# PSUM banks divided into two rings of four, tiled TensorE calls merged, and every engine's call list redrawn

## The reference

```
# 1. state-space block: in-projection, causal convolution over 4 tokens, then per head (8 heads of 64)
z, xBC, dt = split(x @ W_in.T)
y = sum over s<=l of (C_l . B_s) * exp(cum_l - cum_s) * (x_s * dt_s)     # the masked 256x256 matrix Lm
y = (y + x*D) * silu(z);  y = y * rsqrt(mean(y*y)) * norm_w
x1 = layernorm(x + y @ W_out.T)
# 2. attention: queries from x1, keys and values from the 120 context rows and the 256 rows of x1
x2 = layernorm(x1 + softmax(q k^T / 8) v @ Wout)
# 3. coupling network, three cycles, and a global network on the mean over tokens
gf = sigmoid(global_net(mean(x2)))
for 3 cycles: tf = sigmoid(w4 gelu(w3 gelu(w2 gelu(w1 h))));  h = h + coupling(gf, tf) * twist(h)
return layernorm(x2 + h)
```

## Time and profile before

| | |
|---|---|
| median of three runs | 3862.34 us |
| profiled execution: span from first to last instruction | 3861.4 us |
| between span and median | 0.9 us |
| matmul instructions | 25728 |
| TensorE busy | 3783.3 us, 98% |
| VectorE busy | 3286.2 us, 85% |
| ScalarE busy | 3237.9 us, 84% |
| GpSimd busy | 1748.5 us, 45% |
| mean granted TensorE clock | 0.992 of full |

### The profile page before, as it was taken

How to read it: one execution, slowest core, us unless ns; L and a number is a source line. 1 busy time by engine, 2 the same in 40 slices (tenths; PEclk the granted TensorE clock), 3 DMA queues, 4 the chain that set the end, 5 groups by cost and what they waited for, 6 DMA issues and landing times.

```text
span 3861.4 us, 77375 instructions
## 1 busy us (share of the span) xinstructions
PE 3783.3 (98%) x25728; PEld 3000.9 (78%) x25728; DVE 3286.2 (85%) x8098; ACT 3237.9 (84%) x7812; POOL 1748.5 (45%) x3084
## 2 busy tenths in 40 slices
PE   6999999999999999999999999999999999999997
PEld 5777877877877878778778778777787787787775
DVE  7888888888888888888888888888888888888874
ACT  5788888888888888888888888888888888888885
POOL 3444445354454444453544544534535445445442
PEclk8999999999999999999999999999999999999998
DMA  3111112111211111121111111111211211111110
GB/s 97 54 47 59 55 45 61 54 42 58 58 45 55 48 59 54 45 61 53 43 57 59 45 55 50 56 55 45 61 55 42 61 55 45 55 54 53 55 38 17
DMA packets 312350, 203.14 MB, mean 53 GB/s; under 512 B 55056, under 2 KB 310928, under 8 KB 311952
## 3 DMA queue, kind: packets, MB, share of 16 engines
q1 hardware_dynamic: 311952, 198.20, 17.5%
HBM read 180.17 MB, written 17.96 MB: 51 GB/s over the span
## 4 chain that ended last, share of the span: by engine, by line
PE 59%; ACT 16%; DVE 15%; issue 4%; POOL 4%; DMA 1%; SPq 0%; DVEq 0%; POOLq 0%
PE psum L253 20%; PE psum L428 8%; PE psum L338 6%; PE psum L463 5%; PE psum L438 5%; PE psum L452 4%; PE psum L325 4%; ACT prob L979 3%; ACT h L1021 2%; ACT L979 2%; ACT L1021 2%; PE psum L497 2%; ACT xc L891 2%; POOL rs_mix L2175 2%; DVE nmax L1638 1%
## 5 line engine op out<-in xcount | busy, mean ns | idle before, releaser
L979 ACT ACTIVATE prob<-psum,nmax 128x376 f32<-128x376 f32 x1024 | 585.2, 575 | 49.5 <-DVE nmax L1638 46.2
L1638 DVE TENSOR_REDUCE nmax<-psum 128x1 f32<-128x376 f32 x1024 | 541.5, 540 | 14.4 <-PE psum L428 11.0
L2139 POOL TENSOR_TENSOR Lm<-Lm,G 128x384 f32<-128x384 f32 x512 | 506.1, 1012 | 92.8 <-DVE out_sb L1741 68.4
L438 PE MATMUL psum<-ident,prob 128*128 128x128 f32 (+1 forms) x3072 | 480.5, 276 | 2.1 <-ACT probT L989 1.1
L1442 DVE SCALAR_TENSOR_TENSOR u<-psum,par,u 128x253 f32<-128x253 f32 (+5 forms) x960 | 449.1, 479 | 28.1 <-ACT u L882 1.7
L428 PE MATMUL psum<-kT,q_sb 64*128 64x376 f32 x2048 | 467.7, 528 | 0.2 <-ACT prob L979 0.2
L438 PEld LDWEIGHTS psum<-ident,prob 128*128 128x128 f32 (+1 forms) x3072 | 363.0, 141 | 73.9 <-issue 45.0
L989 ACT ACTIVATE probT<-psum 128x384 f32<-128x384 f32 x512 | 252.7, 494 | 182.7 <-PE psum L438 182.5
L2126 POOL TENSOR_SCALAR_AFFINE_SELECT Lm<-Lm 128x256 f32<-128x256 f32 x512 | 205.7, 435 | 411.6 <-DMA Lm<-cum_row 411.6
L253 PE MATMUL psum<-x_hi,w_in_hi 128*128 128x256 f32 (+1 forms) x1152 | 360.9, 313 | 22.5 <-DVE w_in_lo L1764 9.3
L452 PE MATMUL psum<-probT,V 128*64 128x256 f32 (+1 forms) x3072 | 375.0, 385 | 0.3 <-ACT probT L989 0.3
(11 more groups left out here) (222 smaller groups left out, 11157.9 us busy)
## 6 DMA issues: line engine op xcount, KB each, us to landing
Lm<-cum_row SPq DMA_DIRECT2D x64, 1024.0 KB, 5.2
Lm<-cum_row SPq DMA_DIRECT2D x64, 512.0 KB, 6.5
invT<-inv_row SPq DMA_DIRECT2D x256, 128.0 KB, 3.0
xT_sb<-in_xT SPq DMA_DIRECT2D x64, 256.0 KB, 3.1
x_sb<-in_x SPq DMA_DIRECT2D x64, 256.0 KB, 3.3
result<-out_sb SPq DMA_DIRECT2D x64, 256.0 KB, 2.2
inv_row<-inv_t SPq DMA_DIRECT2D x512, 1.0 KB
ctx_sb<-in_ctx SPq DMA_DIRECT2D x64, 120.0 KB, 2.7
```

Of the source, the lines that this page charges most:

```text
L438: t = tr(banks[b][0:m, j * P:(j + 1) * P], prob[:, r, j0:j0 + m], ident[:, :])
L979: act(prob[:, r, :], b[:, 0:NK], ACT.Exp, bias=nmax[:, n:n + 1], accum_out=psum_row[:, n:n + 1]).then_inc(a_exp, 1)
L1638: e.tensor_reduce(nmax[:, n:n + 1], banks[bank_of["sc", s, n]][:, 0:NK], AX.X, ALU.max, negate=True).then_inc(d_max, 1)
L2139: t = tt(Lm[:, h, :], Lm[:, h, :], G[:, :], ALU.mult)
```

## The change

**Banks.** `scores` go round four banks (`RING_S`); every other call of TensorE goes round the other four (`RING_O`), the coupling network included.

**Larger calls.** `scores(s, c)` makes the four products of a head pair in one call instead of two in each of two. `y_half(s, d)` replaces two `y_pair` and puts both results side by side in one bank; `values(s, d)` replaces two `values` likewise. The readers (`y_out` on DVE, `values_out` on ACT) wait until both halves of the bank are written.

**Lists.** All five engines' lists are drawn anew. The loop is still over `p` from 2 to 62, but TensorE's now starts at another point: the second and third cycle of the coupling network of `m - 3` and the last six `turn`s and last `values` of `f` stand at the head of a turn of the loop. The products of all calls are the same, 25728 matmul instructions by the same sizes.

```
-        ring_turn = (4, 5)
+        RING_S, RING_O = (0, 1, 2, 3), (4, 5, 6, 7)
...
-            ring_s, ring_b, ring_m = [1, 2, 3], list(ring_turn), [6, 7]
+            ring_s, ring_o = list(RING_S), list(RING_O)
...
-                b = bank_of["x", s, j] = take(ring_m)
+                b = bank_of["x", s, j] = take(ring_o)
...
-                b = bank_of["tn", s, n] = take(ring_b)
+                b = bank_of["tn", s, n] = take(ring_o)
...
+            def y_half(s, d):
...
+                b = bank_of["y", s, d] = take(ring_o)
                 pe.wait_ge(d_xdt, 2 * s + 2)
+                for q in (2 * d, 2 * d + 1):
+                    pe.wait_ge(l_Lm, 4 * s + q + 1)
+                    o = q % 2 * L
+                    for i, (c0, c1, m0) in enumerate(((0, L, 0), (P, L, L))):
+                        for k in range(2):
+                            h = 2 * q + k
+                            t = mm(banks[b][k * HD:(k + 1) * HD, o + c0:o + c1], xdt[:, i, h * HD:(h + 1) * HD],
+                                   Lm[:, h, m0:m0 + c1 - c0], start=i == 0, stop=i == 1)
+                    t.then_inc(p_y, 1)
+                freed[b] = [(d_yD, 4 * s + 2 * d + 2)]
...
+            def scores(s, c):
...
+                for i in range(TT):
+                    for k in range(2):
+                        n = 2 * (TT * c + i) + k
+                        b = bank_of["sc", s, n] = take(ring_s)
...
+                        freed[b] = [(a_exp, 16 * s + n + 1)]
...
+            def values(s, d):
...
+                for c in (2 * d, 2 * d + 1):
+                    pe.wait_ge(a_tn, 8 * s + 2 * c + 2)
+                    pe.wait_ge(d_tn, 8 * s + 2 * c + 2)
...
+                freed[b] = [(a_o, 4 * s + 2 * d + 2)]
...
-                b = wait_free(0)
+                at = bank_of["f", s, cyc, n] = take(ring_o)
+                b = banks[at]
...
-                sc.wait_ge(p_val, 4 * s + c + 1)
+                sc.wait_ge(p_val, 4 * s + c // 2 * 2 + 2)
...
-                ve.wait_ge(p_y, 4 * s + q + 1)
+                ve.wait_ge(p_y, 4 * s + q // 2 * 2 + 2)
```

More of the change, by code:

```diff
@@ L705, in _ @@
+            layer(last - 3, 1, 2)
+            turn(last - 2, 14)
+            turn(last - 2, 15)
+            layer(last - 3, 1, 3)
+            k_tile(last - 1, 1)
+            k_tile(last - 1, 2)
+            in_z(last, 1)
+            layer(last - 3, 2, 1)
+            q_pair(last - 1, 1)
+            layer(last - 3, 2, 2)
+            values(last - 2, 1)
+            v_tile(last - 1, 0)
             k_tile(last - 1, 3)
+            layer(last - 3, 2, 3)
+            scores(last - 1, 1)
+            turn(last - 1, 0)
@@ L1002, in x2_out @@
                     return
+                b = banks[bank_of["x2T", s]]
                 sc.wait_ge(p_f, FP * s + 1)
```

1479 lines of the change are left out of this document (730 added, 749 removed).

## The result

The changed kernel takes 4058.62 us (median of four runs, 4056.83 to 4061.93) against 3862.67 for the kernel before beside it: a ratio of 1.0507, with a 95% interval of 1.0492 to 1.0522. The direction was forecast, the size was not: 3909 us was the value, 3985 the upper end of the range, and +196 us is over four times the +46 of the sum. The profiled execution has a span of 4055.0 us and a mean granted clock of 0.993.

The account below looks back on a forecast made before the run. TensorE was taken as the bound. Per sequence, -1.35 (visits) + 2.4 (table loads) + 0.3 (banks) - 0.6 (old waits) = +0.75 us, over about 62 sequences +46 us: 3909 us; own range 3870 to 3950, eight in ten 3795 to 3985.

Parts of the forecast that it names:

- TensorE bounds; less work there without new waits is the gain: TensorE is 98% busy at full clock, so the kernel needs less TensorE work per sequence without new waits there.
- Visits, 1.35 us, at most 1.56: Merged scores, values and y calls make fewer trips to half arrays on TensorE, saving 0.96 to 1.56 us per sequence.
- Five loads in one chain, 2.4 us: ScalarE's 10.75 us from in_x to glob(f, 0), against TensorE's 8.39, makes TensorE wait about 2.4 us at glob(f, 1).
- Faster: Rival: TensorE already waits elsewhere in that stretch, halving the glob(f, 1) wait, and visits return their upper price; 3802 us, chance 0.30.
- The four shared banks, 0.3 us, between 0 and 0.6: Calls outside scores wait for the reader of the fourth call before; 0.3 us per sequence allowed, at turn(f, 15).
- the place named as tight: turn(f, 15) takes the bank of turn(f, 12), which DVE reads behind out_norm; 0.3 us, between 0 and 0.6.
- Where readers come at once, nothing waits: At the shared banks, full-array calls between take 0.4 to 1.5 us and a reader 0.5, so no wait.
- Much slower: Rival: the four-bank ring in strict order lets late DVE readers, such as gate_silu, stop TensorE; 3982 us, chance 0.13.
- GpSimd's and the DMAs' other orders, nothing: New orders for POOL, 46% busy, and the DMA queues, 18%, were counted at nothing.
- Old waits go, -0.6 us: TensorE's estimated 0.6 us of true waits per sequence came from the old lists and were counted as gone.
- The signs named in the forecast: mean_square 59.5 us apart, over 1.5 us idle before glob(f, 1), five unbroken loads, scores about 1.5 us, TensorE 94 to 96%.
- The sign of the ring: Sign that the forecast is wrong: idle time spread over many TensorE lines, with readers on DVE as releasers.

Follow-up runs that it names:

- e3: Kernel before with y_pair calls and turns interleaved, so two more visits to half arrays per sequence and the same work: 3912.33 us, ratio 1.0122.
- e15: Kernel before with scores(a, 0, 1) moved ahead of xcT(m, 1), meant to save one visit but leaving 1484 passages as before: 3888.42 us, ratio 1.0062.
- e9: Changed kernel with GpSimd's products Lm<-Lm,G over 16 columns of 384 alone, lists as they were: 3978.4 us, ratio 1.0295.
- e21: Changed kernel with softplus's logarithm as identity, GpSimd's products over 16 columns, and banks exchanged ahead of v_tile(a,0) and mean_square(m): 3872.32 us, ratio 1.0016.
- e10: Control: kernel before with GpSimd's products Lm<-Lm,G over 16 columns alone: 3861.72 us, ratio 0.9990.
- e4c: Kernel before with x2_turn and the coupling network giving up their own bank 0 to share ring (0, 6, 7), lists unchanged: 3966.34 us, ratio 1.0265.
- e20: Changed kernel with the next two shared banks exchanged ahead of v_tile(a,0) and mean_square(m) alone, all work kept: 4022.48 us, ratio 1.0402.

## Why the prediction was wrong, by its own steps

- *TensorE bounds; less work there without new waits is the gain.* Right, and the gain on TensorE was there in full, 2.2 us a sequence.
- *Visits, 1.35 us, at most 1.56.* About right, perhaps a little small: e3 has 0.30 us a visit without its wait for `x_lo`, which makes 1.7, where single rows gave 0.13 to 0.29. The merged `scores` take 1.46 us (1987.36 to 1988.82) and 1.28 by columns, so that a visit still costs 0.18 there. e15 can't bear on it.
- *Five loads in one chain, 2.4 us.* The chain is right to 0.1 us, the wait is 1.6 to 1.7. The subtracted side was wrong: `mean_square` starts 0.93 us late. This is what the rival "Faster" described, two waits side by side, with a bank as the second.
- *The four shared banks, 0.3 us, between 0 and 0.6.* **This step failed.** Three waits of 0.93 us stand there, and `turn(f, 15)`, the place named as tight, is not among them. "Where readers come at once, nothing waits" was true and beside the point: the forecast followed TensorE's list and took the readers' speed for granted, where VectorE's list has `out_norm`, `by_token`, `x1_keep` and `kv_split` ahead of the three readers. The rival "Much slower" named `gate_silu` behind `out_norm` and `by_token`, which is `v_tile(a, 0)` exactly, and had 0.13.
- *GpSimd's and the DMAs' other orders, nothing.* Also failed. GpSimd is 43% busy, and its load said nothing. What counted is which VectorE instruction stands beside it and waits for it: +2.7 us a sequence on VectorE, and 80 us of time where GpSimd's products were left out (e9).
- *Old waits go, -0.6 us.* Of waits over 0.15 us nothing went: 0.88 us stood before, and 0.89 beside the named ones stand after (6.33 less 1.74, 2.80 and 0.90). Smaller pauses did go: the 2.2 us less the visits at 1.6 to 1.7 leave 0.5 to 0.6. Together the two terms were forecast at -1.95 and came to -2.2, so the miss doesn't lie here.

The signs named in the forecast came in part: the wait at `glob(f, 1)`, the five loads and the `scores` of 1.46 us as written, but a period of 62.1 us in place of 59.5 and TensorE's share at 91%, under the 94 to 96. The sign of the ring came too, waits that end with readers on VectorE.

In the forecast's form, per sequence: -2.2 + 1.7 for the tables + 2.8 for the three banks + 0.9 for `xcT` and `y_half` = +3.2 us; 62.14 - 58.93 = 3.21. The parts by experiment: the logarithm's loads 70 us, GpSimd's products 80, two of the bank waits 36; with all three away the kernel is at 3872 us, 186 below the changed kernel and 7 above the kernel before. That doesn't account for all: what the new waits cost is 5.45 us a sequence, the 3.21 and the 2.2 that TensorE saved. e21 still has 3.07 us of waits, 2.2 more than the kernel before, as much as was saved. `xcT`, `bcdt`'s bank at `out_proj` and a number of small ones make them up. `turn(a, 5)`'s wait vanishes with the products, so part of the 80 is a bank's wait, caused by a slow VectorE.

What stays open: the four banks with the old lists, and a private bank for the coupling network with the new ones, weren't tried; as I read the lists, each of these combinations would leave two engines waiting for each other. Leaving the logarithm out of the kernel before, the counterpart of e10, wasn't tried either, so that its 70 us have no control. Hence no run separates "banks" from "lists" altogether; e4c shows that a shared ring costs 102 us with the old lists, the exchanges that two of the new waits are worth 36 with the new ones. No version beat the kernel before. The best one that does all of the work with merged calls is e20, at 4022 us.

## What to carry to other kernels

A wait for a bank is priced from the reader's list, not the writer's: for each call that takes a bank, write down what the previous user's reader has ahead of it on its own engine, and compare that with what stands between the two calls. When two chains end at one engine, subtract them from each other only after asking whether the shorter one starts on time. And a table of idle shares doesn't say that an engine has room: VectorE had 5.8 us of idle gaps in 58.9 and still 2.1 us at the wrong place cost 1.9. Nor is busy time all work: an instruction that takes twice its usual time may be waiting for the engine beside it, which shows when the ends of both are compared.
